# Attention read-out on VectorE instead of ScalarE, and a regrouped order of the FFN stage, in an eight-core transformer kernel

## What is computed

```
x = x + attn_a(LN(x))    # 16 heads of 64, biases on q, k, v, o, a head mask
x = x + ffn(LN(x))       # x @ base.T + 2 * sum over 8 experts of w_e * lora_B_e(lora_A_e(x))
x = x + attn_b(LN(x))    # 16 heads of 64, no biases
x = x + ffn(LN(x))
```

## Time and profile before

| | |
|---|---|
| median of 3 timed runs | 4805.5 us (4804.55 to 5041.72) |
| the profiled execution's own time | 4819.02 us |
| its span, slowest core | 4817.7 us |
| the other cores' spans | 4782.3 to 4809.3 us |
| mean granted TensorE clock, all cores | 0.909 to 0.918 of full speed |

### The profile page before, as it was taken

The page is one execution under the profiler, slowest core; times in us unless marked ns, Lnnn a source line. Parts: engine busy times, 40 slices in busy tenths (PEclk is TensorE's granted clock), DMA queues, the critical chain, the costliest instruction groups (busy, mean ns, idle before and its releaser), DMA issues.

```text
span 4817.7 us, 60181 instructions; the slowest of 8 cores (4782.3 to 4817.7 us)
## 1 busy us (share of the span) xinstructions
PE 3670.8 (76%) x18800; PEld 1363.8 (28%) x18800; DVE 1791.4 (37%) x4025; ACT 2440.4 (51%) x2433; POOL 69.7 (1%) x134
## 2 busy tenths in 40 slices
PE   3888888956688888865556888888567888888657
PEld 1333333212233333321122333332122333333212
DVE  4333333355533333336333222223555322222363
ACT  0477777700057778740002777777100587787400
POOL 0000000000000000000000000000000000000000
PEclk8889999967899999987688999999779999999878
DMA  4000000010100000010122010000101100000101
GB/s 103 9 15 18 12 12 5 5 27 1 31 14 16 12 14 10 10 27 1 70 66 42 12 19 16 12 5 5 27 0 24 22 16 12 16 9 8 27 1 70
DMA packets 33091, 98.81 MB, mean 21 GB/s; under 512 B 5392, under 2 KB 5520, under 8 KB 31248
## 3 DMA queue, kind: packets, MB, share of 16 engines
q0 software_dynamic: 17600, 44.13, 5.8%
q1 hardware_dynamic: 15184, 50.85, 3.1%
HBM read 122.04 MB, written 17.04 MB: 29 GB/s over the span
## 4 chain that ended last, share of the span: by engine, by line
PE 55%; ACT 19%; DVE 8%; issue 7%; DVEq 5%; DMA 5%; ACTq 1%; SPq 0%
ACT s_pbuf L578 18%; PE psC L586 10%; PE psC L593 6%; PE psA L566 5%; DVEq L157 5%; PE psA L795 4%; PE psD L432 4%; PE psE L432 4%; PE psB L566 4%; PE psD L360 4%; PE psE L360 3%; PE psE L533 2%; DMA s_xbuf<-x 2%; PE psD L533 2%; PE psE L468 2%
## 5 line engine op out<-in xcount | busy, mean ns | idle before, releaser
L578 ACT ACTIVATE s_pbuf<-psA,s_negbb 128x1024 bf16<-128x1024 f32 x1024 | 1141.0, 1114 | 592.1 <-PE psA L572 558.9
L578 ACT ACTIVATE s_pbuf<-psB,s_negbb 128x1024 bf16<-128x1024 f32 x1024 | 1140.0, 1113 | 206.3 <-PE psB L572 178.6
L586 PE MATMUL psC<-s_pbuf,s_vaug 128*128 128x512 bf16 x2048 | 785.8, 384 | 383.7 <-ACT s_pbuf L578 327.3
L593 PE MATMUL psC<-s_pbuf,s_vaug 128*128 128x512 bf16 x2048 | 783.8, 383 | 5.0 <-DVE s_sumsT L616 5.0
L360 PE MATMUL psD<-s_bigi,s_xns 128*128 128x512 bf16 x512 | 172.2, 470 | 382.1 <-DVE s_xns L351 382.1
L586 PEld LDWEIGHTS psC<-s_pbuf,s_vaug 128*128 128x128 bf16 x2048 | 195.7, 96 | 929.0 <-issue 929.0
L342 ACT ACTIVATE s_lnv<-s_mv,s_epsb 128x4 f32<-128x4 f32 x32 | 9.4, 294 | 864.9 <-DVE s_mv L338 864.9
L572 PE MATMUL psA<-s_qt,s_kt 64*128 64x512 bf16 x1024 | 400.6, 391 | 0.0
L566 PE MATMUL psA<-s_qt,s_kt 64*128 64x512 bf16 x1024 | 400.6, 391 | 0.0
L566 PE MATMUL psB<-s_qt,s_kt 64*128 64x512 bf16 x1024 | 400.0, 391 | 0.0
L572 PE MATMUL psB<-s_qt,s_kt 64*128 64x512 bf16 x1024 | 400.0, 391 | 0.0
(11 more groups left out here) (124 smaller groups left out, 3794.7 us busy)
## 6 DMA issues: line engine op xcount, KB each, us to landing
s_xbuf<-x SPq DMA_DIRECT2D x32, 512.0 KB, 13.3
s_rexp<-hbm_rr SPq DMA_DIRECT2D x64, 256.0 KB, 3.5
y<-s_xbuf SPq DMA_DIRECT2D x32, 512.0 KB, 2.6
s_wpool<-base POOLq DMA_DIRECT2D x8, 1024.0 KB, 13.3
s_wpool<-wo_a POOLq DMA_DIRECT2D x2, 2048.0 KB, 17.6
s_wpool<-wq_a POOLq DMA_DIRECT2D x16, 256.0 KB, 3.7
s_wpool<-wk_a POOLq DMA_DIRECT2D x16, 256.0 KB, 3.9
s_wpool<-wv_a POOLq DMA_DIRECT2D x16, 256.0 KB, 3.6
```

The source lines that it names most:

```text
L578: P.op("scalar", lambda q, ps=ps, kpar=kpar, hg=hg: q.activation(pbuf[:, kpar * 1024:(kpar + 1) * 1024], ps[:, 0:1024], AF.Exp, bias=negbb ...
L586: P.op("tensor", lambda q, kt=kt, kpar=kpar, par=par: q.matmul(psC[0:128, 0:512], vaug[:, par * NT * 192 + kt * 192:par * NT * 192 + kt * ...
L593: P.op("tensor", lambda q, kt=kt, kpar=kpar, par=par: q.matmul(psC[0:128, 512:1024], vaug[:, par * NT * 192 + kt * 192 + 64:par * NT * 192 ...
```

## The change

Two things are changed.

1. The two copies from psC to aoT at each boundary are made by VectorE (tensor_copy) instead of ScalarE (copy). They stand ahead of the transposes of the sums.
2. The FFN's order is producer(g), consumer(g - 1), producer_b(g), hooks(g - 1). The hook is one function for each tile again; it is called for the four tiles of a group after producer_b, and ends in ln_group at the fourth. So the statistics no longer stand between the x-adds, the LayerNorm of a group comes one round earlier, and the stores and loads at the change of sequence are emitted after the group's consumer (their waits are on the same x-adds as before). For attention, whose last part calls the hook for each tile, the order stays as it was.

```diff
-                P.op("scalar", lambda q, hg=hg, qg=qg: q.copy(
+                P.op("vector", lambda q, hg=hg, qg=qg: q.tensor_copy(
                     aoT[0:64, hg * 2048 + qg * 512:hg * 2048 + (qg + 1) * 512], psC[0:64, 0:512]),
...
-                P.op("scalar", lambda q, hg=hg, qg=qg: q.copy(
+                P.op("vector", lambda q, hg=hg, qg=qg: q.tensor_copy(
                     aoT[64:128, hg * 2048 + qg * 512:hg * 2048 + (qg + 1) * 512],
...
     def make_ln_hook(tag):
-        return Hook(stats=lambda t: ln_tile_stats(tag, t),
-                    group=lambda g: ln_group(tag, g))
+        def hook(t):
+            ln_tile_stats(tag, t)
+            if t % 4 == 3:
+                ln_group(tag, t // 4)
+        return hook
...
-                if hook is not None:
-                    hook.tile(t)
-                    hook.stats(t)
-
-        for g in range(6):
+
+        def hooks(g):
+            if hook is not None:
+                for t in range(g * 4, g * 4 + 4):
+                    hook(t)
+
+        for g in range(5):
             if g < 4:
                 producer(g)
+            if g > 0:
+                consumer(g - 1)
+            if g < 4:
                 producer_b(g)
-            if 1 <= g <= 4:
-                consumer(g - 1)
-            if hook is not None and 2 <= g <= 5:
-                hook.group(g - 2)
+            if g > 0:
+                hooks(g - 1)
...
     def make_last_hook(seq):
-        def tile(t):
+        def hook(t):
             xout_tile(seq, t)
             if seq == 0:
                 xin_tile(1, t)
-        if seq == 0:
-            return Hook(tile=tile,
-                        stats=lambda t: ln_tile_stats("s1.0.ln", t),
-                        group=lambda g: ln_group("s1.0.ln", g))
-        return Hook(tile=tile)
+                ln_tile_stats("s1.0.ln", t)
+                if t % 4 == 3:
+                    ln_group("s1.0.ln", t // 4)
+        return hook
```

More of the change, by code:

```diff
@@ L373, in ln_xnT @@
             ln_group(tag, g)
-    class Hook:
-        def __init__(self, tile=None, stats=None, group=None):
-            self.tile = tile or (lambda t: None)
-            self.stats = stats or (lambda t: None)
-            self.group = group or (lambda g: None)
-    def make_ln_hook(tag):
-        return Hook(stats=lambda t: ln_tile_stats(tag, t),
-                    group=lambda g: ln_group(tag, g))
+    def make_ln_hook(tag):
+        def hook(t):
[3 more added lines that the diff above has]
+        return hook
     def attn_load(kind, tag):
@@ L701, in attn @@
             if hook is not None:
-                hook.tile(t)
-                hook.stats(t)
-                if t % 4 == 3:
-                    hook.group(t // 4)
+                hook(t)
         while tail:
```

3 lines of the change are left out of this document (1 added, 2 removed).

## The result

The changed kernel takes 4992.0 us (median of ten runs, 4921.5 to 5162.0) against 4810.3 of the kernel before; the ratio is 1.026 (95% interval 1.023 to 1.029), so it is slower by 2.6%. The prediction was 4922 us. The median lies above what the ratio gives because in half of the ten executions, and in the profiled one, the cores of one die or of both ran at a lower clock, which the ratio leaves out. Core 0, of the die without it, is read here, and compared with core 0 of the kernel before (4802.0 us); the rows ahead of the prediction are of the slowest core, so their times differ by some us.

A forecast was written before the change was run, and what follows sets the result against it. VectorE's serial order at score-stage boundaries, ahead of the filler eviction TensorE needs, was taken as the path. Attention 137 + clock 28 + FFNs 30 - 66 - 12 = +117 us on 4805.5 gave 4922 us, range 4850 to 4990.

The forecast's parts named there:

- Waits at the boundaries, seven head pairs: Score stages: copies delay VectorE's transposes, chain and filler eviction by 1.5 us, paid less any reserve; 113 us.
- Eighth pairs: Each attention's last head pair, with Wo fillers: three boundaries of 1.45 us and a last of 1.5; 24 us in all.
- The clock: Score stages: longer TensorE waits add one low-clock spell of 1.0 us for each of 28 head pairs; 28 us (0 to 110).
- FFN 1 and 3: FFNs with a LayerNorm behind: new order and bunched statistics cost +15 to +16 us each, +30 together (+5 to +50).
- The 13.8 us gap: FFN, after a consumer: producer_b bare (4.2 us), then copies, four tiles' statistics and norm before the LayerNorm transposes; 13.8 us.
- FFN 2: FFN that stores and reloads x: reloads no longer hold up x-adds, 244 against 310.6 us; -66 us (-45 to -85).
- its last tile: End of FFN 2: last tile's store and load still share DMA engines with attention weights; 26.5 us instead of 8.9.
- FFN 4: Last FFN, without statistics: three rounds save waits, about 9 us, plus about 3 of clock; -12 us.
- The absorbed chain: Rival, score stages: reserve absorbs VectorE's delay except at late-transpose boundaries and the four ends; 4798 us, chance 0.24.
- ScalarE was the path: Rival, score stages: relieving ScalarE of its copies takes 148 us off; 4609 us, chance 0.04.
- The clock falls at most boundaries: Rival, score stages: about 75 boundaries each bring a 1.5 us low-clock spell, 112 us instead of 28; 5006 us, chance 0.14.
- The stores crowding the loads: Rival, FFN 2: stores of x crowd the reloads, so it gains only 30 us; 4958 us, no separate chance given.

The follow-up runs named there:

- e9: Kernel before with only the FFN order changed (producer, consumer, producer_b, LayerNorm group), statistics inline behind each x-add; median 4778.1 us, ratio 0.9935.
- e10: Kernel before, old FFN order, with four tiles' stores, reloads and statistics bunched behind each consumer; no ratio, two shortest executions 4803.7 and 4809.1 us.
- e2: Kernel before with only the two psC-to-aoT copies moved to VectorE, FFN as before; 4960.6 us, ratio 1.0316.
- e4: Kernel before, ScalarE keeping its copies, plus two additional unused VectorE copies of the banks' other quadrants ahead of the transposes; 5012.6 us, ratio 1.0404.
- e5: e2 with VectorE's serial chain behind the transposes cut in four pieces and issued in the next query group; 4844.0 us, ratio 1.0076.
- e6: Kernel before, copies on ScalarE and old FFN, with VectorE's chain cut in four pieces issued in the next query group; ratio 0.9971.
- e3: Kernel before with only the second of the two copies (L610) on VectorE, ScalarE keeping the first; 4925.0 us, ratio 1.0240.

## Why the prediction was right, point by point

The time: 4922 us predicted, 1.026 x 4810.3 = 4935 us by the ratio; 110 us on core 0 against the sum of 117. The path was named rightly, and part of the closeness is luck: the attention's terms came to 150 us instead of 165, the FFNs' to -39 instead of -48, and the two misses take most of each other away.

- **Waits at the boundaries, seven head pairs (113 us of the 137).** Up to Exp 3, summed over the 28 groups of an attention on core 0, the growth is 14.1, 32.2, 34.4 and 24.8 us, 105.5 in all; predicted 21, 32, 33 and 27. The shift of the transposes is 1.44 us (1.5 predicted), the last groups pay 0.16 (0.2). In the first attention the second boundary pays only at Exp 4 (7 x 1.22 = 8.5), so its waits are 22.6 and the sum is 114. In the fourth attention two readings of the reserve missed in opposite directions: the first boundary pays 0.54 us (1.4 predicted), the third 1.81 (0.8).
- **Eighth pairs (24 us).** Measured from the last Exp of the pair's first group on: 3.6, 3.2, 4.0 and 2.8, 13.6 in all. The tails behind them differ by -5 to +5 us one by one and not in sum (600.2 and 599.5 us): the last chain before Wo added nothing. This is the term that was most over-sized.
- **The clock (28 us).** From Exp 3 (Exp 4 there) to the ends: 1.5, -0.4, 15.2 and 5.9, 22 us. I had one more spell of 1.0 us for each head pair everywhere, 28 in all. Their number was right (30 more, 43 instead of 13), their price was 22 us and not 28, and the even spread was wrong: 3, 4, 15 and 8 more by attention. The third attention had the clock at 1.00 throughout and had most to lose: behind two of its boundaries in four the wait now brings a clock of 0.82. In the first two attentions the late-transpose boundary already had its spell (13 of 14), and the longer wait adds none. That is why scores 3 grow by 53.6 us where 46 follow from the terms (33 + 7 + 6).
- **FFN 1 and 3 (+30).** +31.2. The 13.8 us gap came to 13.5 (3.7 for producer_b, 9.78 for the statistics), the last group to 9.0 (8.9). Two steps missed and hid each other. The wait for the softmax chain was put at 2.1 us in each of three consumers, and is 2.1 in all, so that TensorE's idle time in FFN 1 grows by 12.7 us and not by the 19 of the working. The clock was to give back 6 us in the consumers and take 4 in the LayerNorm groups; the consumers' matmuls on xnT (L795, now L789) were busy for 64.1 us instead of 65.8, the transposes (L360) for 41.5 instead of 36.2, TensorE's busy time in the stage grew from 138.8 to 141.8 us, and its granted clock fell from 0.84 to 0.81. (The working's own terms, 57 - 38 - 6 + 4, make 17 for each FFN, 34 for both.) e9 and e10 show the two parts: order -7.5, bunch +23.4.
- **FFN 2 (-66).** -59.1. The step that missed is "its last tile": two reloads, of 13.3 and 11.0 us, stand in a row at the end, and the last gap is 33.2 us, not 26.5. The rest of the stage is what FFN 1 takes, as said: 249.2 - 33.2 = 216.0 against 224.5 - 9.0 = 215.5; the 2 us for the pace were not needed.
- **FFN 4 (-12).** -11.4.
- **The rivals.** The absorbed chain (4798) falls by e2. "ScalarE was the path" falls by e4. "The clock falls at most boundaries" (112 us): it falls at 43 of 84, 30 more than before, and costs 22 us. The stores crowding the loads was not seen beyond the last two tiles.
- **The signs to look for.** Seen: the wait of the first PV pair for the transposes at 85 of 128 boundaries, the FFNs near 225 and 244, no Exp behind a ScalarE copy. The evictions' waits "over 80 us": L465's, for L483, L438 and L445, come to 88 us, from 24. Score stages "longer by 20 to 50": the third is longer by 54.

What the prediction argued for and only e5 and e6 show: that VectorE's order, not its load (39% busy), sets most of the price. With the same copies and the same total work, and the chain out of the way, three quarters of e2's slowdown is gone, and two thirds of what the copies cost against the kernel with the same cut. The last third, some 50 us, stays with the chain moved.

## What to carry to other kernels

An engine that is a third busy can still be the path, where a serial chain on it stands ahead of the one eviction that TensorE's queue needs next: before moving work to it, look at what stands behind that work in its order, and price the shift by the waits that are already there. Put what TensorE waits for (evictions, bank hand-backs) first and what nobody needs soon (sums, statistics) between later steps, in pieces. Waits can cost clock besides: here 0.9 us at a boundary of the third attention whose wait had grown by 1.44 us, and 22 us on some 114 us of waits over the seven head pairs.

## What the runs showed of the hardware

- A wait of TensorE of 1.87 us, where it had been 0.53 us, brought a granted clock of 0.82 in the window behind it and 0.87 us; e3, with a wait of 1.85 us there, had 0.80, and without this wait (e5; the 0.97 us for the transposes stayed) the clock was 1.00. At the 84 boundaries counted above, waits of 1.86 us or more were followed by the lower level in 28 groups of 28, waits of 1.29 to 1.54 us in 14 of 28.
- Splitting two dependent copies over two engines (e3) moves the second engine's queue by 1.32 us, nearly as much as giving it both (1.44): it waits idle for the first.
- VectorE's copy of 64 partitions x 512 fp32 out of PSUM takes 679 to 695 ns, and VectorE's copy of 128 partitions 682 ns; ScalarE's of 64 takes 578 to 581 ns. In e4 both engines read at the same time, other quadrants of the same banks, and each stays within 20 ns of that.
